# Scattering the dense edges in node order, 460 of the 508 scatters in setup and 48 in the first layer, with 40 dense blocks ahead of the pairs

## The reference

```python
h = relu(layernorm(x))
for i in range(3):                      # layers of the first network
    msg = relu(h[src]) + 1e-7
    out = softmax_aggregate(msg, dst) + h     # exp-weighted mean of msg over the edges of a node
    h = relu(W2[i] . relu(batchnorm(W1[i] . out + b1[i])) + b2[i])
x = x + h
x = x + second_network(layernorm(x), edge_attr, src, dst)   # three layers of node and edge linears
```

## Time and profile before

| | us |
|---|---|
| median of three runs | 4172.19 |
| the profiled execution | 4165.19 |
| its span, first to last instruction | 4163.4 |
| PE busy | 3299.3 (79%) |
| POOL busy | 2373.3 (57%) |
| DVE busy | 2217.1 (53%) |
| ACT busy | 1941.5 (47%) |

### The profile page before, as it was taken

How to read it: one execution, slowest core, us unless ns; L and a number is a source line. 1 busy time by engine, 2 the same in 40 slices (tenths; PEclk the granted TensorE clock), 3 DMA queues, 4 the chain that set the end, 5 groups by cost and what they waited for, 6 DMA issues and landing times.

```text
span 4163.4 us, 70803 instructions
## 1 busy us (share of the span) xinstructions
PE 3299.3 (79%) x19961; PEld 2595.9 (62%) x19961; DVE 2217.1 (53%) x5689; ACT 1941.5 (47%) x3697; POOL 2373.3 (57%) x2488
## 2 busy tenths in 40 slices
PE   2287777769898789888699888758788888888887
PEld 0144444458777677777577777746666666666665
DVE  6144333325444555445665445736666666666666
ACT  0222111146555576555585555734444444444444
POOL 2666666646666366666356665255565565565552
PEclk6588988889999899999899999879999999998988
DMA  7155433467777367777367776554444444444442
GB/s 291 54 184 191 138 119 120 124 202 246 248 235 236 117 231 234 251 234 242 110 230 243 243 235 197 151 160 126 124 129 129 127 128 128 128 125 127 127 125 63
DMA packets 419116, 713.14 MB, mean 171 GB/s; under 512 B 75585, under 2 KB 259067, under 8 KB 416098
## 3 DMA queue, kind: packets, MB, share of 16 engines
q0 software_dynamic: 130688, 321.08, 26.0%
q1 hardware_dynamic: 270119, 323.45, 25.5%
q10 hardware_dynamic: 18107, 66.24, 4.2%
HBM read 561.11 MB, written 149.39 MB: 171 GB/s over the span
## 4 chain that ended last, share of the span: by engine, by line
PE 36%; another core or an unknown queue 18%; issue 14%; DVE 14%; ACT 10%; DVEq 2%; ACTq 2%; DMA 1%; SPq 1%; POOL 0%; POOLq 0%
PE ps L1570 17%; PE ps L1593 4%; ACT casts L1466 2%; PE ps L718 2%; DVE acc L2369 2%; DVE acc L2403 2%; PE ps L2242 2%; DVE onehot L2396 1%; PE ps L2221 1%; ACTq L934 1%; DVE acc L2396 1%; PE ps L712 1%; ACT two_parts L1456 1%; PE ps L700 1%
## 5 line engine op out<-in xcount | busy, mean ns | idle before, releaser
L2211 POOL DMA_INDIRECT ring<-h_table,idx_ring x832 | 815.9, 981 | 563.2 <-issue 272.9
L652 POOL DMA_INDIRECT pair_rings<-split_table,src_idx x728 | 713.6, 980 | 409.8 <-issue 202.5
L1570 PE MATMUL ps<-casts,two_parts 128*128 128x500 f32 (+1 forms) x3464 | 823.1, 391 | 141.4 <-DVE two_parts L1660 73.8
L1570 PEld LDWEIGHTS ps<-casts,two_parts 128*128 128x128 f32 x3464 | 646.3, 198 | 280.2 <-DVE two_parts L1660 83.5
L665 POOL DMA_INDIRECT adjacency<-acc x508 | 495.8, 976 | 344.4 <-issue 144.7
L1660 DVE TENSOR_TENSOR two_parts<-work,two_parts 128x512 fp32r<-128x512 f32 (+1 forms) x276 | 187.4, 679 | 588.9 <-ACT two_parts L1456 349.8
L1466 ACT ACTIVATE casts<-spare 128x1000 fp32r<-128x1000 fp8e4 (+1 forms) x471 | 458.9, 974 | 8.5 <-PE ps L1570 4.8
L2308 ACT ACTIVATE work<-acc,vecs 128x512 f32<-128x512 f32 x208 | 150.2, 722 | 562.4 <-DVE acc L2369 303.5
L1456 ACT ACTIVATE two_parts<-work 128x512 fp32r<-128x512 f32 (+1 forms) x276 | 169.7, 615 | 452.8 <-remote 232.5
L2221 PE MATMUL ps<-ident,ring 128*128 128x128 f32 x1664 | 292.3, 298 | 83.6 <-issue 59.2
L2260 PEld LDWEIGHTS ps<-mats,work 128*128 128x128 f32 x1664 | 238.2, 204 | 141.7 <-issue 140.4
(11 more groups left out here) (333 smaller groups left out, 6242.6 us busy)
## 6 DMA issues: line engine op xcount, KB each, us to landing
spare<-adjacency SPq DMA_DIRECT2D x216, 250.0 KB
acc<-e_few SPq DMA_DIRECT2D x208, 256.0 KB
work<-msg_table SPq DMA_DIRECT2D x144, 256.0 KB
work<-in_edge_attr SPq DMA_DIRECT2D x104, 256.0 KB
e_few<-spare SPq DMA_DIRECT2D x52, 512.0 KB
spare<-rel_rows SPq DMA_DIRECT2D x208, 84.0 KB
spare<-adjacency SPq DMA_DIRECT2D x72, 187.5 KB
e_few<-work SPq DMA_DIRECT2D x26, 512.0 KB
```

Source lines behind the costliest of these rows:

```text
L652: e.indirect_dma_start(out=to, out_offset=None, in_=table, in_offset=bass.IndirectOffsetOnAxis(ap=src_idx[:, 2 * i + h, j:j + 1], axis=0)) ...
L1570: ins = e.matmul(bank, parts_of(d)[:, b % 2, q, kind * D:(kind + 1) * D], cast_counts[n % CASTS][:, at:at + width], start=opens, stop=(b = ...
L2211: e.indirect_dma_start(out=rows[:, s, j, :], out_offset=None, in_=h_table, in_offset=bass.IndirectOffsetOnAxis(ap=idx_ring[:, s, j:j + 1], ...
```

## The change

The edges that the scatters write are dealt out in another order. Before, partition p held 508 edges in a row (COLS), so each scatter touched destination nodes of every region. Now they come in four segments of 127 columns (WIDE): segment s holds the s-th quarter of the edges, so that the scatters go through the nodes in order, and the first quarter writes only to the first two regions. With this:

- ACT clears two regions (6 transfers), then loads x, then clears the other two and the rest of `msg_table`. The first scatter waits for the first two regions alone, scatter 127 for the rest.
- The address work on DVE has 4 x (127 + 78) = 820 columns where it had 508 + 78 = 586, and the 39 comparisons have 4 x (127 + k) where they had 508 + k.
- Setup issues 460 scatters (EARLY). The other 48 are issued by POOL at the start of the first layer's edges phase, ahead of its pair gathers. There the third group of four waits until 3 dense blocks are done, the next until 6, and so on to 30. SP waits for all of them before it loads the first counts of the third region.
- In the first layer 40 dense blocks stand in eight steps (-8 to -1) ahead of the first pair, five in a step, and the other 156 are spread evenly over the 42 steps of the pairs, by their number of columns. The other two layers keep their order.
- The places and counts of the scatters have SBUF tensors of their own, since the edges phase would write over them.

```diff
+SEGMENTS = 4
+WIDE = COLS // SEGMENTS
+REACH = WIDE + 2 * NEAR
+EARLY = 460
+LEAD = 8
+LEAD_BLOCKS = 40
-def step_of(n):
+def step_of(layer, n):
     r, b = divmod(n, BLOCKS)
+    columns = [sum(widths) for _, widths in REGIONS]
+    before = sum(BLOCKS * w for w in columns[0:r]) + b * columns[r]
+    if layer == 0:
+        lead = sum(columns[k // BLOCKS] for k in range(LEAD_BLOCKS))
+        if n < LEAD_BLOCKS:
+            return n * LEAD // LEAD_BLOCKS - LEAD
+        return (before - lead) * PAIRS // (BLOCKS * sum(columns) - lead)
...
-        def scatters(e, S):
-            e.wait_ge(S("zero_fill"), 16 * FILLS * len(REGIONS))
-            e.wait_ge(S("addresses"), 1)
-            for i in range(COLS):
+        def scatters(e, S, first, end):
+            for i in range(first, end):
                 n = i // EACH
+                if i == 0:
+                    e.wait_ge(S("zero_fill"), 16 * FILLS * 2)
+                if i == WIDE:
+                    e.wait_ge(S("zero_fill_rest"), 16 * (FILLS * (len(REGIONS) - 2) + 1))
                 if i % EACH == 0 and n >= SCATTERS:
                     e.wait_ge(S(f"gather_spread{n % SCATTERS}"), 16 * EACH * (n // SCATTERS))
-                if i % EACH == 0:
+                if i % EACH == 0 and i < EARLY:
                     reached(e, S("few_e0"), 2 * pairs_behind(n))
+                if i % EACH == 0 and i >= EARLY:
+                    reached(e, S("dense"), 3 * (n - EARLY // EACH - 1))
...
             def pool(e, S):
                 setup_pool(e, S)
-                scatters(e, S)
-                scattered(e, S)
+                e.wait_ge(S("addresses"), 1)
+                scatters(e, S, 0, EARLY)
+                scattered(e, S, EARLY)
...
+                    for r in range(2):
+                        clear(r)
                 for k in range(5):
                     at = slice(k * PART, (k + 1) * PART)
                     by_sixteens(e, x_rows[:, at, :], ...)
+                if not again:
+                    for r in range(2, len(REGIONS)):
+                        clear(r)
...
+                    if ready and d == 2 * DUOS:          # SP, edges phase
+                        scattered(e, S, COLS)
...
             def pool(e, S):                              # edges phase
+                if ready:
+                    scatters(e, S, EARLY, COLS)
                 for i in range(PAIRS):
...
-                for i in range(PAIRS + 3):               # PE; ACT and DVE likewise
-                    blocks = [n for n in range(ALL_BLOCKS) if step_of(n) == i]
+                for i in range(-lead, PAIRS + 3):
+                    blocks = [n for n in range(ALL_BLOCKS) if step_of(layer, n) == i]
```

More of the change, by code:

```diff
@@ L83, in chunks_before, with blocks_halfway @@
     return sum(len(widths) for _, widths in REGIONS[0:r])
-def step_of(n):
+def step_of(layer, n):
     r, b = divmod(n, BLOCKS)
+    columns = [sum(widths) for _, widths in REGIONS]
[5 more added lines that the diff above has]
+        return (before - lead) * PAIRS // (BLOCKS * sum(columns) - lead)
     if r == 0:
         return b * FIRST_STEPS // BLOCKS
[L91 to L98, removed]
+    first = BLOCKS * columns[0]
+    return FIRST_STEPS + (before - first) * (PAIRS - FIRST_STEPS) // (BLOCKS * sum(columns) - first)
+def blocks_halfway(layer, i):
+    steps = [step_of(layer, n) for n in range(BLOCKS * len(REGIONS))]
     return sum(s < i for s in steps) + sum(s == i for s in steps) // 2 if i in steps else 0
@@ L140, in dense_jobs @@
             for n in range(width // CH):
-                jobs.append((step_of(BLOCKS * (r + 1) - 1) + 3, CUT + at + n * CH, chunks, False))
+                jobs.append((step_of(layer, BLOCKS * (r + 1) - 1) + 3, CUT + at + n * CH, chunks, False))
             at += width
-    out, now = [], -1
+    out, now = [], -LEAD - 1
     for ready, node, least, sparse in sorted(jobs):
@@ L147, in dense_jobs @@
     return out
-JOBS = [j for j in dense_jobs() if j[0] < PAIRS - 1]
-LATE = [j for j in dense_jobs() if j[0] >= PAIRS - 1]
+JOBS_OF = [[j for j in dense_jobs(layer) if j[0] < PAIRS - 1] for layer in range(L)]
+LATE = [j for j in dense_jobs(0) if j[0] >= PAIRS - 1]
 FIRST_OF_LAST = CHUNKS - len(REGIONS[-1][1]) + 1
@@ L765, in addresses_dve @@
             e.wait_ge(S("counted"), NEAR)
-            then(e.tensor_scalar(count_8.bitcast(F8), later, 1.0, None, ALU.add, saturate=False))
+            then(e.tensor_scalar(in_segments(count_8.bitcast(F8)), later, 1.0, None, ALU.add, saturate=False))
             then(e.tensor_scalar(spread_f, earlier, 0.0, None, ALU.is_gt))
@@ L922, in act, with clear @@
             def act(e, S):
+                def clear(r):
+                    width = PITCH if sum(REGIONS[r][1]) > PITCH // 8 * 7 else sum(REGIONS[r][1])
+                    rows = adjacency[r * SPAN * PITCH:r * SPAN * PITCH + NR * PITCH, :].rearrange("(p b d) o -> p b (d o)", b=BLOCKS, d=PITCH)
+                    for h in range(FILLS):
+                        at = slice(h * BLOCKS // FILLS, (h + 1) * BLOCKS // FILLS)
+                        n = at.stop - at.start
+                        zeros = Z0[:, 0:-(-n * width // 4)].bitcast(U8)[:, 0:n * width].rearrange("p (b d) -> p b d", d=width)
+                        e.dma_start(rows[:, at, 0:width], zeros).then_inc(S("zero_fill" if r < 2 else "zero_fill_rest"), 16)
                 if not again:
@@ L1295, in edges_phase @@
             columns = iota_w[:, :]
+            lead = LEAD if ready else 0
+            JOBS = JOBS_OF[layer]
             by_node = [work[0:WW, b, 0:2 * D] for b in range(2)]
@@ L1341, in duos_at @@
             def duos_at(i):
-                return [d for d in range(ALL_DUOS) if step_of(first_block(d)) == i + 1]
+                return [d for d in range(ALL_DUOS) if step_of(layer, first_block(d)) == i + 1]
             def blocks_of(u):
@@ L1355, in evacuated @@
             def evacuated(i):
-                return [r for r in range(len(REGIONS)) if step_of(BLOCKS * (r + 1) - 1) + 1 == i]
+                return [r for r in range(len(REGIONS)) if step_of(layer, BLOCKS * (r + 1) - 1) + 1 == i]
             def jobs_of(i):
```

105 lines of the change are left out of this document (53 added, 52 removed).

## The result

The changed kernel takes 4199.34 us (median of 8 runs, 4193.88 to 4214.43) against 4172.98 for the kernel before (8 runs): ratio 1.0065, 95% interval [1.0040, 1.0089]. It is slower by 0.65% where I had forecast 0.3% faster.

What follows compares the result with a forecast made beforehand. Neither PE nor POOL was taken to bound the kernel throughout; POOL would bound the changed first layer's pairs. Terms -19 - 17 + 25 - 2 = -13 us gave 4159 against the median 4172.2, range 4120 to 4195.

Steps and rivals of the forecast that it cites:

- Front of setup: Setup up to the attribute loop: earlier first scatter, x and ACT work save 15 to 21 us, taken as 19.
- rival B: Setup's stalled stretch shrinks, the attribute loop starts near 135 in place of 172; 4128 us, chance 0.15.
- Scatters out of setup: End of the attribute loop: the last 16 pairs go at 4.32 us without scatters beside them, saving 17 us.
- Rival C: Setup: only the front gains, the attribute loop's last 16 pairs keep 5.4 us each; 4176 us, chance 0.20.
- Scatters and blocks ahead of the pairs: Start of the first layer: 48 scatters, paced by waits for blocks, end 91.6 us after the phase's start.
- The step that failed: the pairs: First layer's 42 pairs, bound by POOL at 11.0 us each, 462 us; the layer's POOL part 25 us longer.
- rival A: First layer: POOL's cadence of 11.75 us a pair holds whatever PE does, slower at 4190 us; chance 0.27.
- Behind the last gather: End of the first layer: the 23 us after the last gather get 2 us shorter.
- All after it: Layers two and three keep the same steps: 0 us, bounds -2 to 2.

Runs made afterwards that it cites:

- e3: Changed kernel with the 48 scatters' waits on dense blocks left out, the 40 blocks still ahead of the pairs; 1.0117 of the kernel before (4226.63 us).
- Half_blocks: Changed kernel with half of PE's work in the 156 blocks beside the first layer's pairs left out; 1.0012 of the kernel before, 11.56 us a pair.
- front_loaded: All scatters in setup, the added wait, 147 first-layer blocks in 24 steps and 49 narrower ones in 18; 0.9954 of the kernel before.
- the four corners: Old block order or 40 blocks ahead: 0.9931 or 1.0088 with 508 scatters in setup, 0.9994 or 1.0117 with 48 in the layer without waits.
- even_no_lead: All scatters in setup, no blocks ahead, the first layer's 196 blocks spread evenly over its 42 steps; 0.9976 of the kernel before.
- the added wait: POOL's first four gathers of each pair also wait for all blocks of the step two before; on the kernel before 0.9960, on the changed kernel 1.0027.

## Why the prediction was wrong

**Front of setup** (-19): -16.6 by the first L738. The first scatter at 53.4 was forecast as 53, and x was there for DVE at 56.4, forecast as 57. For ACT I had 15 to 19 us, since the late clearing would block its issues until 70 to 73; they held it until 82.8, and it gained 4.7. The number held because the front ended behind POOL's row, which was done 20.3 us earlier, less the 3.8 us by which the loop followed later behind it. The stalled stretch did not shrink: the attribute loop's first matmul (L700 before, L720 now) comes at 177.4 in place of 194.7, where rival B wanted under 150. So rival B falls. The Trainium skill, DMA: Bandwidth & Descriptors (Queues, rings and completion order), has each DMA engine take turns between its queues; by that rule the front would have gained 5 us more than 19. It gained less, so the rule gave the chain nothing here; whether the engines took turns these rows don't tell.

**Scatters out of setup** (-17): POOL's first instruction of the layer stands at 827.15, forecast as 827.5, so setup in all gained 36.3 against 36, and this term is -36.3 + 16.6 = -19.7. That is more than the bound of 17, by which PE goes no faster than 4.32 a pair: once POOL was still, the last pairs took 4.0 (63.3 us over 15.75 pairs, forecast about 69 for all). Rival C falls.

**Scatters and blocks ahead of the pairs** (91.6 us from the phase's start): 918.64 - 827.15 = 91.5. No long gaps on PE, as I had counted; e3 shows that this hung on the waits.

**The step that failed: the pairs.** "Neither end is shown for such a step; the row nearest to it is 11.75, but its pause has less to wait for. I take 11.0. 42 x 11.0 = 462". It measured 505.7, 12.04 a pair: 44 us more, and the whole miss of the sum is 42 (-13 forecast, +28.7 measured). Every other term lies within 3 us of its forecast. The argument took the pause for a wait that gets shorter when PE is done sooner. But the earlier trace rows showed the opposite already, and rival A says so in words: the pause stood where PE had been done microseconds before. Half_blocks (11.56) and the last steps of front_loaded (12.10) show that it hardly shrinks with PE's work. With rival A's 11.75 the sum gives 4190; with 12.04 it gives 4202, where 4199 was measured. Rival A, with a chance of 0.27, came nearest, and is right in kind but not in detail: of the 505.7 us, by POOL's time line, the 336 issues take 434 (1.29 each) and waits of over 1 us 72, 20 of them of about 2 us, where A has one in nearly every pair, and five of 3 to 10 us, the 10.45 above among them. My 11.0 left 28 us for all waits.

**What I had not seen.** The earlier trace rows hold it: in the first eight steps of before, PE does 49 blocks in 102 us *while* POOL does its pairs at nearly its own pace. Those blocks were almost free, and the change moved 40 of them ahead, where they stand beside nothing but 48 scatters, and thinned the rest below what fits beside a pair. The price of that is the 1.2 to 1.6% of the four corners; with all scatters in setup even_no_lead splits it, 0.45% for an even spread alone and 1.1% more for putting 40 of the blocks ahead. In the changed kernel PE's earlier start (39.7 us) hid more than half of the 71.1 us that the layer lost.

**Behind the last gather** (-2): 22.8 against 23.2, -0.3. **All after it** (0): the shift of 31.4 at the last sum is 28.7 at the end of the span, -2.7, just past the bound of 2. In all: -39.7 + 71.1 - 2.7 = +28.7.

**A better version.** The cheap part of the change is worth having: four segments, two regions cleared first, x ahead of the rest, all scatters in setup, the old order of blocks: 0.9931. With the added wait it is 0.9918 and 0.9910 on two chips (4145.79 and 4182.65 us, against 4174.38 and 4221.68), with a wait for every two gathers 0.9900 (4182.87 against 4226.22). Each beats both kernels; among themselves they can't be told apart.

## What to carry to other kernels

Before work is moved off a busy engine, find out by the rows who paces the loop: halve each engine's part once, and see which of the two halvings shortens a step. Relief given to an engine that doesn't pace the loop comes back as idle time and, in these rows, as a lower clock. Work that runs beside a fixed-pace row of another engine is nearly free while it fits into a step of that row; the same work ahead of the row is paid for in full.

Count the indirect DMAs as a cost on all engines, not on POOL alone, and give their row a wait now and then for a current count of the engine that it feeds.

## What the runs showed of the hardware

- Without its 508 scatters of 128 bytes setup was 274 us shorter (849.3 - 575.6), 0.54 us for each; the two were run on different chips, and the one without on the slower.
- A count of PE reached ACT and DVE 14 us late beside 16 back-to-back gathers, and ACT stood for 23 us beside an unbroken row of scatters. Released: 1.5 us after POOL stopped in the one case, 1.4 us after scatters gave way to gathers in the other. What holds the counts back no view shows.
- A further wait of POOL for blocks of two steps before made the kernel before 0.4% faster [0.2%, 0.6%].
- PE's granted clock was lower where PE had idled: 1.00 in the stretches where it was over 99% busy, 0.77 to 0.93 where it was 61 to 84% busy. The same 350 or so matmuls were 86.9 us busy at 0.86 against 82.3 at 0.97.
